# Moving the mask multiply of the keys from VectorE to GpSimd in the last cross attention

## The reference

```python
Q = (query @ Wq.T + bq).reshape(b, sq, H, D).transpose(0, 2, 1, 3)     # x: 4 batches of 512 rows
K = (key @ Wk.T + bk).reshape(b, sk, H, D).transpose(0, 2, 1, 3)       # context: 4 batches of 1601 rows
V = (value @ Wv.T + bv).reshape(b, sk, H, D).transpose(0, 2, 1, 3)
Q = apply_rope(Q, cos_q, sin_q)
K = apply_rope(K, cos_k, sin_k)                                        # x * cos + x2 * sin
scores = jnp.einsum('bhqd,bhkd->bhqk', Q, K) * SCALE
scores = jnp.where(mask[:, None, None, :] == 0, neg_inf, scores)       # mask over the 1601 keys
attn = jax.nn.softmax(scores, axis=-1)
```

## Time and profile before

| | |
|---|---|
| median of 3 runs | 1927.8 us (1926.09 to 1930.58) |
| profiled execution, first to last instruction | 1928.0 us |
| PE busy over the span | 1765.4 us (92%) |
| DVE busy | 1407.8 us (73%) |
| ACT busy | 1062.6 us (55%) |
| POOL busy | 712.1 us (37%) |

### The profile page before, as it was taken

The page is one execution under the profiler, slowest core; times in us unless marked ns, Lnnn a source line. Parts: engine busy times, 40 slices in busy tenths (PEclk is TensorE's granted clock), DMA queues, the critical chain, the costliest instruction groups (busy, mean ns, idle before and its releaser), DMA issues. The chain is left out here.

```text
span 1928.0 us, 34145 instructions
## 1 busy us (share of the span) xinstructions
PE 1765.4 (92%) x13236; PEld 984.1 (51%) x13236; DVE 1407.8 (73%) x2375; ACT 1062.6 (55%) x1722; POOL 712.1 (37%) x789
## 2 busy tenths in 40 slices
PE   8999999989999999789999888599999999999786
PEld 4787577668888888432333454212222222223354
DVE  2524788757777776776777289989999999994563
ACT  1221555535555555235666443178888888886442
POOL 0654977025555554242331134313332121202442
PEclk9999999999999999977999999689999999999898
DMA  5134999776666665441110357411201010100001
GB/s 193 51 102 145 306 316 329 273 267 255 251 252 255 253 250 188 126 137 26 27 35 19 125 159 223 123 45 56 79 19 36 19 33 21 35 2 1 25 12 33
DMA packets 114324, 245.89 MB, mean 128 GB/s; under 512 B 28282, under 2 KB 83102, under 8 KB 110688
## 3 DMA queue, kind: packets, MB, share of 16 engines
q1 hardware_dynamic: 87204, 204.66, 30.8%
q0 software_dynamic: 24848, 36.95, 7.1%
q10 hardware_dynamic: 2112, 2.10, 0.3%
HBM read 180.77 MB, written 62.30 MB: 126 GB/s over the span
## 5 line engine op out<-in xcount | busy, mean ns | idle before, releaser
L2076 DVE TENSOR_REDUCE Eh_maxima<-Eh_max 128x2 f32<-128x802 f32 x512 | 474.7, 987 | 21.6 <-PE Eh_max L1955 16.8
L2064 ACT ACTIVATE Eh_probs<-Eh_pair 128x1024 f32<-128x1024 f32 (+1 forms) x288 | 287.5, 998 | 113.3 <-PE Eh_pair L1994 113.3
L1436 PE MATMUL C_y<-C_x_high,C_W 128*128 128x256 f16 x1472 | 251.0, 274 | 1.5 <-DVE C_x_low L1676 1.5
L1955 PE MATMUL Eh_max<-Eh_KS,Eh_QS 49*128 49x401 f16 x1024 | 197.5, 357 | 45.9 <-DVE Eh_maxima L2076 42.0
L2017 PE MATMUL Eh_av_ps<-Eh_probs,E_V 128*17 128x512 f32 (+1 forms) x1664 | 223.7, 610 | 0.0
L1436 PE MATMUL C_y<-C_x_low,C_W 128*128 128x256 f16 x736 | 201.8, 274 | 0.0
L2076 DVE TENSOR_REDUCE Dh_maxima<-Dh_max 128x2 f32<-128x1024 f32 x128 | 152.1, 1221 | 49.2 <-PE Dh_max L1963 47.3
L2064 ACT ACTIVATE Eh_probs<-Eh_single 128x512 f32<-128x512 f32 x272 | 161.7, 594 | 28.7 <-PE Eh_single L1994 28.7
L1955 PEld LDWEIGHTS Eh_max<-Eh_KS,Eh_QS 49*128 49x128 f16 x1024 | 50.3, 94 | 234.3 <-DVE Eh_maxima L2076 201.3
L1793 POOL DMA_DIRECT2D Eh_KS<-E_kd x64 | 37.1, 579 | 351.0 <-PE Eh_pair L1994 346.2
L1436 PEld LDWEIGHTS C_y<-C_x_high,C_W 128*128 128x128 f16 x1472 | 144.8, 98 | 19.0 <-issue 1.7
(11 more groups left out here) (422 smaller groups left out, 3633.9 us busy)
## 6 DMA issues: line engine op xcount, KB each, us to landing
C_W<-w_split SPq DMA_DIRECT2D x23, 3072.0 KB, 11.5
w_split<-B_w_parts SPq DMA_DIRECT2D x24, 768.0 KB, 9.2
Eh_KS<-E_kd POOLq DMA_DIRECT2D x64, 150.1 KB, 3.3
C_tail<-in_expert_tail_dram SPq DMA_DIRECT2D x23, 384.0 KB, 8.4
B_places<-in_w_experts_dram SPq DMA_DIRECT2D x10, 768.0 KB, 6.6
A_QT<-in_w_experts_dram SPq DMA_DIRECT2D x8, 768.0 KB, 5.1
w_split<-A_QT SPq DMA_DIRECT2D x8, 768.0 KB, 6.6
early_more<-in_w_experts_dram SPq DMA_DIRECT2D x8, 768.0 KB, 11.5
```

The lines of the kernel that those rows point to most:

```text
L1436: last = mm(y_ps[n % Y_BANKS][:, i, :], W[:, u, a, at_w:at_w + P], x[:, s % 2, k, :], start=(q == 0), stop=(q == len(parts) - 1))
L1955: last = self.nc.tensor.matmul(bank[:, a, 0:self.cw], self.QS[r, slot, p, qt * P:(qt + 1) * P], self.KS[r, slot, p, k0:k0 + self.cw], star ...
L2064: self.nc.scalar.activation(dst, src, ACT.Exp, scale=1.0 / SCORE).then_inc(self.exp_done, 1)
L2076: self.nc.vector.tensor_reduce(self.maxima[:, g % 2, :, p * TPB + qt, c], self.max_ps[n % 2][:, :, 0:self.cw], AX_X, ALU.max).then_inc(sel ...
```

## The change

DVE no longer multiplies by the mask factors. POOL does it (`keys_kept`), in the same buffer, and it does it one item ahead: it multiplies item n+1 before it lowers item n. For a query item `keys_kept` only waits for the sum and passes the signal on. `E_t` gets a third buffer (`SUMS = 3`), so DVE waits for the lowering of item n-3 instead of n-2. To make room, the weights and the statistics of the output projection before this stage live in `E_other`, which is not in use by then.

```diff
+SUMS = 3
-        t, other = sb("t", [P, 2, 2, S]), sb("other", [P, 2, S])
+        t, other = sb("t", [P, SUMS, 2, S]), sb("other", [P, 2, S])
-        after = OutProjection(own, nc, "Do", X, XT, ATT, ident, dram["self_WoT"], None)
+        after = OutProjection(own, nc, "Do", X, XT, ATT, ident, dram["self_WoT"], None, W=other[:, 0, :].rearrange("p (k d) -> p k d", d=D),
+                              stats=other[:, 1, 0:NT * 6].rearrange("p (t s) -> p t s", s=6))
...
+            def keys_kept(n):
+                b, kn, c0, w = part_of(n)
+                pool.wait_ge(summed, n + 1)
+                if kn is None:
+                    pool.wait_ge(kept, n)
+                    pool.sem_inc(kept, 1)
+                else:
+                    tt(t[:, n % SUMS, :, 0:w], t[:, n % SUMS, :, 0:w], keep[:, kn % 2:kn % 2 + 1, 0:w].broadcast_to([P, 2, w]), ALU.mult).then_inc(kept, 1)
...
+            keys_kept(0)
             for n in range(ITEMS):
-                pool.wait_ge(kept, n + 1)
+                if n + 1 < ITEMS:
+                    keys_kept(n + 1)
                 lower(n)
                 if n - QUERY_PLACES[0] - 2 in (0, 1):
                     first_loads(n - QUERY_PLACES[0] - 2)
...
-                if n >= 2:
-                    dve.wait_ge(low_ready, n - 1)
+                if n >= SUMS:
+                    dve.wait_ge(low_ready, n - SUMS + 1)
...
-                dve.wait_ge(summed, n + 1)
-                if kn is None:
-                    dve.sem_inc(kept, 1)
-                else:
-                    v.tensor_tensor(t[:, n % 2, :, 0:w], t[:, n % 2, :, 0:w], keep[:, kn % 2:kn % 2 + 1, 0:w].broadcast_to([P, 2, w]),
-                                    ALU.mult).then_inc(kept, 1)
```

More of the change, by code:

```diff
@@ L33, with __init__ @@
 class Norm:
-    def __init__(self, ctx, nc, name, X, eps, side=None):
+    def __init__(self, ctx, nc, name, X, eps, side=None, stats=None):
         self.nc, self.X, self.eps = nc, X, eps
@@ L42, in __init__ @@
         sem = lambda n: ctx.enter_context(nc.semaphore(f"{name}_{n}"))
-        self.stats_buf = sb("stats", [P, NT, 6])
+        self.stats_buf = sb("stats", [P, NT, 6]) if stats is None else stats
         self.mv = sb("mv", [P, NT, 2])
@@ L2124, with __init__ @@
 class OutProjection:
-    def __init__(self, ctx, nc, name, X, XT, ATT, ident, WoT, bias, side=None):
+    def __init__(self, ctx, nc, name, X, XT, ATT, ident, WoT, bias, side=None, W=None, stats=None):
         self.nc, self.X, self.XT, self.ATT, self.ident, self.WoT, self.bias, self.name = nc, X, XT, ATT, ident, WoT, bias, name
@@ L2130, in __init__ @@
         sb = lambda n, shape: ctx.enter_context(nc.sbuf_tensor(f"{name}_{n}", shape, F32, side=side))
-        self.norm = Norm(ctx, nc, f"{name}_norm", X, LN_EPS, side)
+        self.norm = Norm(ctx, nc, f"{name}_norm", X, LN_EPS, side, stats)
         self.loaded, self.turned, self.copied = sem("loaded"), sem("turned"), sem("copied")
         self.out_ready, self.sum_ready, self.turned_back, self.copied_back = sem("out_ready"), sem("sum_ready"), sem("turned_back"), sem("copied_back")
-        self.W = sb("W", [P, KD, D])
+        self.W = sb("W", [P, KD, D]) if W is None else W
         self.need = 16
@@ L2835, in high @@
                         act.wait_ge(stored[n % 2][m], 16 * (n // 2))
-                nc.scalar.copy(parts[:, n % 2, 0, :, 0:w], t[:, n % 2, :, 0:w]).then_inc(high_ready, 1)
+                nc.scalar.copy(parts[:, n % 2, 0, :, 0:w], t[:, n % SUMS, :, 0:w]).then_inc(high_ready, 1)
             for c in range(2):
@@ L2873, in lower @@
                 pool.wait_ge(high_ready, n + 1)
-                tt(parts[:, n % 2, 1, :, 0:w], t[:, n % 2, :, 0:w], parts[:, n % 2, 0, :, 0:w], ALU.subtract).then_inc(low_ready, 1)
+                tt(parts[:, n % 2, 1, :, 0:w], t[:, n % SUMS, :, 0:w], parts[:, n % 2, 0, :, 0:w], ALU.subtract).then_inc(low_ready, 1)
+            def keys_kept(n):
[6 more added lines that the diff above has]
+                    tt(t[:, n % SUMS, :, 0:w], t[:, n % SUMS, :, 0:w], keep[:, kn % 2:kn % 2 + 1, 0:w].broadcast_to([P, 2, w]), ALU.mult).then_inc(kept, 1)
             def first_loads(a):
@@ L2923, in first_vector @@
                 for m in range(2):
-                    v.scalar_tensor_tensor(t[:, n % 2, m, 0:w], pair_ps[n % 2][:, m, 0:w], bias[:, m:m + 1],
+                    v.scalar_tensor_tensor(t[:, n % SUMS, m, 0:w], pair_ps[n % 2][:, m, 0:w], bias[:, m:m + 1],
                                            rotary[:, 2 * m, c0:c0 + w], ALU.add, ALU.mult)
@@ L2929, in first_vector @@
                 dve.wait_ge(rotated, n + 1)
-                v.tensor_tensor(t[:, n % 2, :, 0:w], t[:, n % 2, :, 0:w], other[:, :, 0:w], ALU.add).then_inc(summed, 1)
-                dve.wait_ge(summed, n + 1)
-                if kn is None:
-                    dve.sem_inc(kept, 1)
-                else:
-                    v.tensor_tensor(t[:, n % 2, :, 0:w], t[:, n % 2, :, 0:w], keep[:, kn % 2:kn % 2 + 1, 0:w].broadcast_to([P, 2, w]),
-                                    ALU.mult).then_inc(kept, 1)
+                v.tensor_tensor(t[:, n % SUMS, :, 0:w], t[:, n % SUMS, :, 0:w], other[:, :, 0:w], ALU.add).then_inc(summed, 1)
     with ExitStack() as own:
```

## The result

| | before | after |
|---|---|---|
| median, us (19 runs each, same chip) | 1926.09 | 1933.41 |
| lowest to highest | 1920.71 to 1935.95 | 1927.23 to 1937.68 |
| ratio to before | | 1.0030, 95% 1.0016 to 1.0043 |

The changed kernel is slower by 0.3%, 5.8 us with 3.1 to 8.3 as the interval. (The ratio is estimated from all runs; the two medians alone are 7.3 us apart.) The forecast was 1936 us, 8.3 us above 1927.8, the median of the three runs of before that were known then.

The account below looks back on a forecast made before the run. DVE (4.49 us an item) was put only 0.1 us above PE (4.39), so late stores would decide. Three chains, +2.4, +4.1 and +1.8, gave +8.3 on 1927.8: 1936 us, forecast's own range 1931 to 1942, 8 in 10 1921 to 1942.

Parts of the forecast that it names:

- The second chain: Item 9 to item 15: lowerings, stores, landing and the cast of item 13 put item 15 at 34.7 us, +4.1.
- The third chain: Item 15 to the maxima: late context puts item 19 +3.9 us later, faster DVE behind it gives -2.1; together +1.8.
- The first: Up to item 9: item 5 lowered only after item 6's sum delays stores and the cast of item 7; +2.4 us.
- The multiply on GpSimd: Time of the moved multiply on POOL, taken from the lowering's rows: 1.64 us narrow, 1.9 us wide.
- the order decides by itself: POOL lowers item n only after item n+1's sum and multiply; this decides, with DVE saving and third buffer costed at nothing.
- DVE was the bound and PE's waits go: Rival: PE's waits vanish but the first, and the last multiply: -11.6 us, 1916 us; faster had chance 0.17.
- Its break-even at a landing of 2.6 us: Three chains hold one store or load landing each; they cost 8.3 us at 5.4, nothing at 2.6, below which it wins.
- Landings near 3.6: Rival: DMA landings near 3.6 us instead of 5.4 leave +2.9 us, 1931 us; no change had chance 0.16.
- Sums held through two POOL operations: Rival: DVE sums wait 1.64 us for each of two POOL operations; +14.5 us, 1942 us; no chance of its own.
- POOL's multiply is dear: Rival: multiply takes 2.6 us instead of 1.64 in second and third chains; +2.9, 1939 us, within the forecast (0.62).
- Context before item 19 by about 5 us: Sign the forecast is right: PE waits about 5 us for context before item 19.
- DVE less by 16 us: Sign the forecast is right: DVE's busy time in the key and query stage falls by 16 us, idle time instead.

Follow-up runs that it names:

- e1_not_ahead: Changed kernel, but GpSimd lowers each item before it multiplies the next, never one ahead; 4.4 us above before (0.4 to 8.5).
- e2_buffers_only: Kernel before plus only the third sum buffer and the output projection's weights and statistics in `E_other`; VectorE multiplies; -2.9 us against before (-5.6 to -0.4).
- e10_order_only: Kernel before with three sum buffers, VectorE multiplying, and GpSimd lowering item n only when n+1 is multiplied; 9.2 us above before (6.0 to 12.3).
- e5: Changed kernel with its late order, but the multiply by the kept keys left out; +0.8 us against before (-2.7 to 4.0).
- e11: Changed kernel with the multiply left out and each item lowered at once, three sum buffers; -5.4 us against before (-7.1 to -3.7).
- e3: Changed kernel, with mask and context loads issued before the wait for the lowering; +6.2 us against before (2.5 to 9.8).
- e8: Kernel before, weights in `E_other`, with one extra unused GpSimd multiply behind every lowering but the last; +17.1 us against before (12.7 to 21.6).

## Why the prediction came out right, and which step was wrong

**The sum held, chain by chain.** Up to item 9: +2.4 said; the stretch from 7 to 9 grew by 3.2 and the one before by 0.3. Between 9 and 15: +4.1 said, +4.6 measured. From 15 to 19: +3.9 said, +2.7 measured. Behind it: -2.1 said, -2.15 measured. Sum 8.3 said, 8.7 in the profiled stage, 5.8 by the ratio of all runs. That the stage's gain or loss is the kernel's does not hold for the profiled pair, whose spans are 3.5 us apart.

Inside them the steps can be followed. The second chain said 22.6 us from item 9 to the end of the lowering of 10, it was 23.4; the second stores of 11 at 26.3, they were issued at 26.9; the cast of 13 at 31.7, it was 32.2; item 15 at 34.7, it was 35.2. The lowering of item 10 is the missing part:

```profile
1181.63 1.56 POOL L2885 TENSOR_TENSOR E_t<-E_t,E_keep 128x768 f32<-128x768 f32 x1
1183.13 2.64 POOL L2876 TENSOR_TENSOR E_parts<-E_t,E_parts 128x768 f16<-128x768 f32 x1
```

```profile
1182.55 1.73 DVE L2943 TENSOR_TENSOR E_t<-E_t,E_other 128x1024 f32<-128x1024 f32 x1
```

The lowering took 2.64 us instead of 1.64, and ended 1.49 behind this sum of DVE, which stood there before it.

The third chain was said 1.2 us too long, by its landing: the context of item 19 was issued 16.9 us behind item 15 (17.0 said) and landed in 4.3, not 5.4. The columns of this row of DMAs from 1203 to 1225 are KB and us to landing:

```profile
E_halves<-ctx_parts SPq DMA_DIRECT2D x1, 449.0 KB, 4.3
```

The first was said too short, by PE's clock. The cast of item 7 came at 35.97 us behind item 2 (36.1 said), but from it to item 9 it took 4.38 us instead of 3.04. The 24 matmuls of the last values ran at half the clock (columns as in the earlier trace rows; the third row is the wide item 14 of before):

```profile
1156.80:1162.00 5.20, 5.20 (x24) 3.59 (x24) 2.20 (x2) 2.51 (x6) 4.17 (x3) 0.50 0.57 180
...
1188.30:1193.10 4.80, 4.68 (x12) 1.63 (x12) 1.17 (x3) 1.99 (x5) 2.59 (x2) 0.50 0.97 274
```

```profile
1184.10:1187.00 2.90, 2.46 (x12) 1.09 (x12) 2.83 (x6) 0.48 (x1) 0.00 (x0) 1.00 0.79 246
```

Granted 0.50, that is 1.2 GHz instead of 2.4. PE had waited 3.33 us before the one and 5.64 before the other. The wide item of before, behind a wait of 2.45 us, took 2.46 us at full clock, and so did item 19 of the changed kernel behind 3.12 us. The second of the slow groups did not delay item 15, since the cast of item 13 set that. The prediction priced waits only.

**The multiply on GpSimd** was taken at 1.64 and 1.9 us and measured 1.65 and 1.78: not dear.

**The step that failed**, though the time came out inside the range, is the claim that the order decides by itself: that all which counts is that POOL lowers an item only behind the next item's sum, with the DVE saving and the buffers costed at nothing. e1_not_ahead hasn't this order and still takes 7.3 us more than e2_buffers_only, which has the same buffers. What the prediction had not priced is that the multiply on POOL delays lowerings without the order too, from 3.7 to 6.2 us behind the sum. e10_order_only has the order alone and costs 12.1 us more than e2, where order and move together cost 8.7. So VectorE's multiply is not free in the late order: with it (e10) the kernel takes 8.4 us more than with nobody multiplying (e5); with the multiply on POOL it takes 5.0 more, though there the intervals overlap. And the buffers, e2, came out at -2.9 us. That the sum was near the result is owed to having timed the chains of the changed kernel itself, and in part to luck, since the clock, the landing and the buffers stood in no term and partly cancel. It would have misjudged the version without the order.

**The rivals.** *DVE was the bound and PE's waits go*: e11 gains 5.4 us, of which e2's buffers have 2.9, so about 2.5 were to be had, not 11.6, and the two intervals overlap. Its break-even at a landing of 2.6 us rested on the chains alone and was not put to the test; e1, in which landings hold one cast (3.6 us), is slow too, which speaks against it. *Landings near 3.6*: the three landings on the chains took 4.7, 5.2 and 4.3 us, between the cases. *Sums held through two POOL operations*: it happened once in the stage, at 1175.92 (below), and was taken up by item 14, where DVE waited 3.63 us for PE. *POOL's multiply is dear*: no.

**Signs named ahead.** Stores of item 5 behind the sum of item 6: yes. PE waiting for ACT before the last values of items 8 and 14: 3.33 and 1.10 us. Context before item 19 by about 5 us: 3.12; the 5.64 stood before item 14. DVE less by 16 us: 12.5 in the stage; the 20 sums together took 3.8 us more than in before. Casts released by DMAs: yes, for 12 of the 20.

## What to carry to other kernels

An engine that is busy 90% of a stage may be relieved of a sixth of its work for little gain (2.5 us here, not clear of noise), when the next engine in line is 0.1 us an item behind; so price a moved step at each place where it lengthens a chain of buffers coming free (sum, cast, lowering, store, next cast), and price the same step where it stands today as well, not at nothing. A software-pipelined order ("one ahead") on an in-order engine delays everything queued behind the later half (12.1 us here by itself); try the order and the move apart before they are put together. A wait that is removed can have another right behind it: e3 took 8.8 us of waits from PE and got 9.0 others.

## What the runs showed of the hardware

A sum of DVE can be shut out through two GpSimd instructions in a row. Both engines of the changed kernel around 1176:

```profile
1175.09 1.66 POOL L2885 TENSOR_TENSOR E_t<-E_t,E_keep 128x768 f32<-128x768 f32 x1
1176.69 2.14 POOL L2876 TENSOR_TENSOR E_parts<-E_t,E_parts 128x1024 f16<-128x1024 f32 x1
```

```profile
1175.92 3.73 DVE L2943 TENSOR_TENSOR E_t<-E_t,E_other 128x768 f32<-128x768 f32 x1
```

The sum began 0.8 us into the multiply and ended 0.8 us behind the lowering, though the lowering began later than it. The same happened in e3 (3.75 us) and e8 (3.54). It does not always go so: the sum at 1182.55 of the changed kernel (above) also stood behind a multiply with a lowering next, but took 1.73 us, and it was the lowering that was held (2.64 us, above). In all, the 20 sums of the changed kernel were held 6.4 us over their bare lengths (0.96, 1.10 and 1.23 us by shape), against 2.6 in before. And an operation of DVE with one SBUF input is not safe: making `keep` from the mask, 0.36 us, took 1.79 beside GpSimd at 1184.20 of the changed kernel, and 2.32 beside a lowering in before:

```profile
1187.77 2.32 DVE L2901 TENSOR_SCALAR E_keep<-E_mask 128x449 bf16<-128x449 int32 x1
```

```profile
1187.71 2.14 POOL L2874 TENSOR_TENSOR E_parts<-E_t,E_parts 128x1024 f16<-128x1024 f32 x1 [5.62 <-ACT E_parts L2836]
```

The Trainium skill (SBUF — State Buffer, Who interferes with whom) lets whoever issues first have the shared pair for the whole instruction. For the lowering of 2.64 us the trace agrees; for the sum of 3.73 us it does not, since by the records the sum stood there 0.77 us before the lowering began.
